# A vision-transformer tower on one core: image tiles asked for at the start and pooled between the parts of the weight preparation, the two layers' weights turned behind the first planes

## The chip, the cores and the metric

The kernel runs on 1 core of one Trainium2 chip, in one launch. The metric is the device time of that launch in microseconds (us), the median of several runs. Engine names: PE or TensorE (matmul), DVE or VectorE, ACT or ScalarE, POOL or GpSimd, SP or SyncE (here it only issues DMAs). ACT issues DMAs too: x tiles go on ACT's queue, all else on SP's.

## The reference

64 images of 12 channels, 224 x 224, float32. Each image becomes T = 196 tokens (14 x 14 patches) of width D = 192, goes through one attention layer over the whole width, a residual, and then an expert layer with its own attention of 12 heads:

```python
pooled = x.reshape(B, C, 14, 16, 14, 16).sum(axis=(3, 5))         # 12 values a token
h = einsum('bcij,ce->bije', pooled, channel_weights)
h = h + attn(layernorm(h), Wq, bq, Wk, bk, Wv, bv)                 # softmax over 196 tokens
# expert layer on layernorm(h): router -> softmax -> top 98 of 196 tokens for each of 4 experts
h1 = expert_sum(mask_e * (layernorm(y) * gamma + beta)) @ w1.T + b1      # 768 hidden + 3 x 192
x_attn = attention(12 heads, q, k, v from h1);  x_mlp = gelu(h1[:768])
out = y + combine(mask_e * (concat(x_mlp, x_attn) @ w2.T + b2)) , the two halves of w2's rows added
```

Since a token is made of 12 values, the kernel folds the weights together first (`Abd`, `WR`, `G4`, `WI` for the first attention, `M` for the product with w1) and works on 25 numbers per token up to `M`.

## The kernel before, in words

**Stages.** The program has a preparation, a prologue for the first group of 8 images, a loop over the groups, and two closing sections. Every engine runs its own list of operations in order, written from tables of (slot, operation): `prologue()`, `opening()` and `body()` make them, and `run` (L601) walks them for each engine. An operation is a pooling piece, a planes product, one round of choosing, and so on. The loop's table (`body`) is the same in both kernels.

**Preparation.** SP asks for 20 weight loads (L652 to L671), w1 (960 KB and a rest of 48 KB), w2 (1440 KB) and the two biases last, all counted on one semaphore `w_in`. PE waits for all 20 and turns the weights with transposes: Wq, Wk, Wv, the router, the centred channel weights, w1 (22 transposes), the summed halves of w2 (16), through four PSUM banks that ACT empties (L739, L1028). Then come small products: `banks[0]` and `banks[1]` from cwcT (L727, L732), the second of which is `Vp`. ACT copies Vp out, SP copies it into the middle rows of `G` with a DMA from SBUF to SBUF (L673; the rows call it hid<-hid), and DVE centres G into `Gc` (L1212 to L1214). PE turns Gc, multiplies it (L744 to L751), DVE makes `A_rep`, `S_rep`, `L` (L1216 to L1229), PE spreads them (L755 to L761), and DVE writes `Abd`, `WR`, `G4`, `WI` (L1234 to L1241). Last, PE multiplies L with the turned w1 into four banks (L767, L769) and ACT copies them out as `M` (L1035). SP waits for the turned w2 and sends the summed b2 as a bias row into w2T (L676, semaphore `bias_in`), and PE waits for M, for DVE's last piece and for bias_in ahead of anything else.

**Tiles of x.** Each group of 8 images is 12 tiles of 1568 KB (112 partitions), loaded into three buffers in turn (`xt`, NX = 3). `load` (L1050) asks for the first three on ACT's queue, behind M's copies; `fetch` (L1055) asks for tile n + 3 when tile n is pooled. DVE pools a tile in seven pieces (`pool`, L1260, reduction at L1267). POOL spreads the sums of a tile (`own_row`, L1513). After three tiles, which are a pair of images m, PE gathers them (`planes`, L786), ACT copies the result, PE makes tokens (`tok`, L796) and DVE copies these (`tok_raw`, L1274). Tiles of the next group are pooled in pieces set between the operations of this one.

**Routing.** After the fourth tok: a layer norm whose power is taken by POOL (L1522, three times), the first attention image by image (first_max L819 and L1308, first_exp L835, first_mix L844), the stream (L853 to L868), the gates (L1361 to L1384), a turn (`gate_rows`, L876, copied to `rows` at L1390), 13 rounds of choosing the 8 largest (L1398, L1403), `chosen`, `spread` (u_tok, L1420 and L1423; the rows call it both<-zs,sel) and `turn_u` (L892). Then the opening: project (L919), hidden for all 8 images (L909), and the first image's 12 peaks (L937 on PE, L1459 on DVE, two banks), and then the loop.

A table entry of the prologue is written like this (m is the pair, t the tile, p the piece):

```python
    for m in range(GRP // PAIR):
        front += pooling(0, m, steadily(TILES * PIECES * m, 1))
    end = TILES * PIECES * GRP // PAIR + 3
    ...
    for m in range(AHEAD):
        front += pooling(1, m, steadily(end + 6 + 0.75 * TILES * PIECES * m, 0.75))
```

## Time and profile before

| what | value |
|---|---|
| median of 3 runs | 1855.82 us (1848.53 to 1863.67) |
| the profiled execution | 1857.67 us |
| its span in the trace | 1855.8 us, 34563 instructions |
| busy PE, PEld, DVE, ACT, POOL | 1525.9, 1252.8, 1215.5, 846.7, 249.2 us |
| chain that ended last | PE 37%, DVE 26%, issue 21%, DMA 7% |
| DMA | 218.03 MB, 117 GB/s in the mean |

Times in rows count from the span's start. PEld is the weight load of a matmul and overlaps PE. In a timeline a row is a start, a busy time, engine and line, the operation, output <- input, how many, and in brackets the idle time before it with what ended it. In the table of windows the columns are named in the rows' group. The granted clock (PEclk) is a share of TensorE's full clock: 1.00 is the level of 2.4 GHz and 0.50 that of 1.2 GHz. The idle time of an engine that nothing waits for costs nothing.

### The profile page before, as it was taken

The numbers are of one execution on the slowest core, as the hardware profiler recorded it, in microseconds if no ns is written. First come the engines' busy times: TensorE is split into PE (matmuls) and PEld (weight loads), VectorE is DVE, ScalarE is ACT, GpSimd is POOL, SyncE is SP. The second block draws the span as 40 slices with busy tenths as digits, with TensorE's granted clock in tenths as the row PEclk, the third lists the DMA queues.
The fourth block names the chain that finished last, engine by engine and source line by source line (L and its number), as shares of the span: only waits on it lengthen the run. The fifth ranks groups of instructions, "written<-read, shape, count | busy, mean of one in ns | idle before, by whom it ended". The sixth has DMA issues, their size and how long they took to land.

```text
span 1855.8 us, 34563 instructions
## 1 busy us (share of the span) xinstructions
PE 1525.9 (82%) x12440; PEld 1252.8 (68%) x12440; DVE 1215.5 (65%) x2822; ACT 846.7 (46%) x1935; POOL 249.2 (13%) x318
## 2 busy tenths in 40 slices
PE   4214188998889898998899898989989899989998
PEld 3103176777777677777777677867777687868786
DVE  3366847785877657784877667784777757573552
ACT  1001054544545455544645455544545456545653
POOL 2002101220012001210012001120022101110000
PEclk8556578999999899998999899997899899999999
DMA  3797635542656155542646155642656152101220
GB/s 77 198 231 186 182 82 143 142 131 64 173 128 175 49 150 145 145 128 71 174 128 166 49 154 141 155 121 57 162 137 173 49 150 50 41 25 43 54 57 15
DMA packets 99598, 218.03 MB, mean 117 GB/s; under 512 B 61371, under 2 KB 75877, under 8 KB 88678
## 3 DMA queue, kind: packets, MB, share of 16 engines
q10 hardware_dynamic: 12288, 154.15, 31.5%
q1 hardware_dynamic: 87142, 61.68, 14.4%
q8 instruction: 102, 1.67, 0.4%
q14 instruction: 66, 0.54, 0.1%
HBM read 186.57 MB, written 28.90 MB: 116 GB/s over the span
## 4 chain that ended last, share of the span: by engine, by line
PE 37%; DVE 26%; issue 21%; DMA 7%; POOL 4%; ACT 3%; SPq 0%; DVEq 0%; ACTq 0%; POOLq 0%
DVE psums L1267 9%; DVE peaks L1459 6%; PE bank L1002 6%; PE bank L909 5%; PE bank L971 4%; DMA xt<-in_x_dram 4%; PE bank L919 3%; POOL var L1522 3%; PE bank L937 3%; DMA qs<-shiftT 3%; PE bank L956 2%; PE bank L835 2%; PE bank L819 2%; DVE rows L1403 2%; DVE top L1398 1%
## 5 line engine op out<-in xcount | busy, mean ns | idle before, releaser
L1459 DVE TENSOR_REDUCE peaks<-bank 98x2 f32<-98x392 f32 x768 | 424.6, 562 | 185.8 <-PE bank L937 164.9
L1155 ACT ACTIVATE Pb<-bank 98x392 f32<-98x392 f32 x768 | 374.7, 497 | 290.7 <-PE bank L956 250.1
L1267 DVE TENSOR_REDUCE psums<-xt 112x2 f32<-112x512 f32 x672 | 430.1, 678 | 74.7 <-DMA xt<-in_x_dram 52.6
L937 PE MATMUL bank<-ks,qs 96*98 96x196 f16 x1536 | 265.4, 259 | 59.5 <-DMA ks<-qk_scratch 31.6
L1002 PE MATMUL bank<-w2T,hid 128*98 128x192 f32 x1536 | 301.9, 335 | 0.0
L956 PE MATMUL bank<-qs,ks 97*98 97x196 f16 x1536 | 267.0, 258 | 9.9 <-DMA qs<-shiftT 9.2
L937 PEld LDWEIGHTS bank<-ks,qs 96*98 96x98 f16 x1536 | 165.8, 127 | 143.0 <-DVE peaks L1459 50.4
L1002 PEld LDWEIGHTS bank<-w2T,hid 128*98 128x98 f32 x1536 | 240.3, 170 | 1.7
L971 PE MATMUL bank<-Pb,vals 98*32 98x196 f32 x3072 | 181.5, 357 | 11.6 <-ACT Pb L1155 11.6
L956 PEld LDWEIGHTS bank<-qs,ks 97*98 97x98 f16 x1536 | 167.5, 130 | 20.1 <-DMA qs<-shiftT 10.7
L1448 DVE TENSOR_TENSOR qk<-bank,qk 96x392 f16<-96x392 f32 x128 | 71.8, 561 | 137.9 <-ACT qk L1142 129.5
L1550 POOL TENSOR_TENSOR fin<-fin,both 98x384 f32<-98x384 f32 x64 | 63.8, 997 | 651.9 <-DVE fin L1484 651.9
L909 PE MATMUL bank<-UT,M 104*128 104x196 f32 x768 | 143.6, 338 | 0.0
L909 PEld LDWEIGHTS bank<-UT,M 104*128 104x128 f32 x768 | 132.6, 197 | 2.6 <-issue 2.2
L971 PEld LDWEIGHTS bank<-Pb,vals 98*32 98x32 f32 x3072 | 84.5, 114 | 72.5 <-issue 48.1
L1133 ACT ACTIVATE hid<-bank 128x392 f32<-128x392 f32 x192 | 93.9, 497 | 83.0 <-PE bank L909 82.5
L1513 POOL TENSOR_TENSOR spread_p<-psums,cst 112x196 f32<-112x196 f32 x96 | 49.9, 520 | 595.7 <-DVE psums L1267 595.3
L786 PE MATMUL bank<-spread_p,cst 112*24 112x196 f32 x192 | 49.2, 406 | 97.9 <-POOL spread_p L1513 97.9
L1067 ACT COPY oT<-bank 128x196 f32<-128x196 f32 x192 | 61.9, 322 | 132.0 <-PE bank L971 127.1
L1002 PE MATMUL bank<-w2T,onT 96*98 96x192 f32 (+1 forms) x512 | 106.7, 331 | 8.5 <-ACT onT L1067 8.5
L919 PE MATMUL bank<-UT,M 104*96 104x196 f32 x512 | 111.8, 368 | 0.1
L786 PEld LDWEIGHTS bank<-spread_p,cst 112*24 112x24 f32 x192 | 20.4, 120 | 118.2 <-issue 112.4
(181 smaller groups left out, 1826.2 us busy)
## 6 DMA issues: line engine op xcount, KB each, us to landing
xt<-in_x_dram ACTq DMA_DIRECT2D x96, 1568.0 KB, 8.9
qk_scratch<-qk SPq DMA_DIRECT2D x64, 294.0 KB, 4.1
qs<-qk_scratch SPq DMA_DIRECT2D x192, 73.5 KB, 2.9
ks<-qk_scratch SPq DMA_DIRECT2D x192, 73.5 KB, 3.0
out_dram<-fin SPq DMA_DIRECT2D x64, 147.0 KB
qs<-shiftT SPq DMA_DIRECT2D x128, 2.3 KB
hid<-in_L_ffn_w_dram SPq DMA_DIRECT2D x1, 1440.0 KB
hid<-in_L_ffn_w_dram SPq DMA_DIRECT2D x1, 960.0 KB
```

Of the source, the lines that this page charges most:

```text
L786: mm = pe.matmul(ps[0:PAIR * C, 0:T], const("plane", PP)[:, PAIR * C * t:PAIR * C * t + PAIR * C], spread_p[:, t, :, :].rearrange("p a b - ...
L909: mm = pe.matmul(ps[:, T * j:T * j + T], M[:, 128 * f:128 * f + 128], UT[:, i, :], start=True, stop=True)
L919: mm = pe.matmul(ps[0:DC, T * c:T * c + T], M[:, f:f + DC], UT[:, i, :], start=True, stop=True)
L937: mm = pe.matmul(peak_ps[s][0:HT, T * q:T * q + T], qs[0:KS, i % NSTACK, h, HT * q:HT * q + HT], ks[0:KS, i % NSTACK, h, :], start=True, s ...
L956: mm = pe.matmul(score_ps[s][0:HT, T * k:T * k + T], ks[:, i % NSTACK, h, HT * k:HT * k + HT], qs[:, i % NSTACK, h, :], start=True, stop=True)
L971: mm = pe.matmul(ps[32 * j:32 * j + 32, 0:T], vals[:, i % 2, q, h, :], Pb[:, (H * i + h) % NP, q, :], start=(q == 0), stop=(q == 1))
L1002: mm = pe.matmul(misc_ps[slot][0:HT, D * h:D * h + D], lhs, w2T[0:w, f, :], start=(f == 0), stop=(f == NF + 1))
L1133: act.activation(hid[:, i, 2 * b:2 * b + 2, :].rearrange("p a b -> p (a b)"), ps[:, 0:2 * T], ACT.Gelu).then_inc(free, 1)
L1155: act.activation(Pb[:, (H * i + h) % NP, :, :].rearrange("p a b -> p (a b)"), score_ps[s][0:HT, 0:2 * T], ACT.Exp, scale=float(DH) ** -0.5 ...
L1267: last = dve.tensor_reduce(psums[:, m % 2, t, 2 * p:2 * p + 2], v[:, 2 * p:2 * p + 2, :, :], AX.XY, ALU.add)
L1448: dve.tensor_tensor(qk16[:, m, 1, :, :].rearrange("p c t -> p (c t)"), misc_ps[slot][0:DC, 0:2 * T], qk16[:, m, 0, :, :].rearrange("p c t ...
L1459: dve.tensor_reduce(peaks[:, h // 6, :, h % 6], peak_ps[s][0:HT, 0:2 * T].rearrange("p (q k) -> p q k", q=2), AX.X, ALU.max, negate=True). ...
```

## The change

What it does:

- Tile 0 of x is asked for as ACT's first act, tiles 1 and 2 when the 15 small weight loads are in. `w_in` now counts 15 loads, and the five of w1, w2, b1, b2 have a semaphore of their own (`w12_in`). Tiles 3, 4 and 5 are asked for by SP, tile 3 ahead of the copy of Vp into G and the other two behind it, each when a buffer has been pooled. `load` is gone.
- DVE pools tile 0 ahead of its first preparation step, tile 1 behind Gc, tile 2 behind L. Its functions for the operations are moved ahead of the preparation in the file, unchanged.
- The turning of w1 and w2 and the products for M leave the preparation and become an operation `fuse` of three parts, which PE and ACT do in the prologue behind the planes of the pairs 0, 1 and 2, and DVE (the sum over w2 and b2) in part 0. They use the score and peak banks. The tok of the first three pairs comes later in the table, behind the fuse.
- SP sends the bias row when all late turns are done. PE waits for M in project and hidden of the prologue and for the bias in hidden.
- The next group's first two pairs are pooled at other slots of the routing, the third within the opening; turn_u comes where the choosing ends.

The core of the diff ("..." marks what is left out):

```diff
-W_LOADS = 20
+W_LOADS = 15
+W12_LOADS = 5
 REPLACED = -1.0
...
-    ops = [("load", 0)]
     front = []
+    pieces = TILES * PIECES
     for m in range(GRP // PAIR):
-        front += pooling(0, m, steadily(TILES * PIECES * m, 1))
-    end = TILES * PIECES * GRP // PAIR + 3
+        for slot, op in pooling(0, m, steadily(pieces * m, 1), True, 1.2 if m == GRP // PAIR - 1 else 7):
+            if op[0] not in ("pool", "fetch") or (op[0] == "pool" and TILES * m + op[3] >= SETUP_TILES) \
+                    or (op[0] == "fetch" and TILES * m + op[3] >= SETUP_TILES):
+                front.append((slot, op))
+    front += [(pieces * (m + 1) + 4, ("fuse", 0, m)) for m in range(3)]
+    end = pieces * GRP // PAIR + 3
     first, at = routing(0, end)
     front += first + [(at + 0.5 * r, ("choose", 0, r)) for r in range(ROUNDS)]
     front += choosing(0, at + 0.5 * ROUNDS + 1)
-    for m in range(AHEAD):
-        front += pooling(1, m, steadily(end + 6 + 0.75 * TILES * PIECES * m, 0.75))
-    front += turning(0, end + 60)
-    return ops + in_order(front) + sum(opening(0, False), [])
+    front += pooling(1, 0, steadily(end + 9, 0.95))
+    front += pooling(1, 1, steadily(end + 29, 0.65))
+    plan = [in_order(front + turning(0, at + 0.5 * ROUNDS + 3))] + opening(0, False)
+    for slot, op in in_slots(pooling(1, 2, steadily(1, 0.24))):
+        plan[min(slot, len(plan) - 1)].append(op)
+    return sum(plan, [])
...
+            sp.wait_ge(pooled, 1)
+            sp.dma_start(xt[:, 0, :], x_tile(0, NX)).then_inc(x_in[0], 16)
             sp.wait_ge(su_act, 2)
             sp.dma_start(G[C:2 * C, :], Vp).then_inc(su_dma, 16)
-            sp.wait_ge(turn_free, NT - 1)
-            sp.wait_ge(su_dve, 4)
+            for t in range(NX + 1, NX + SETUP_TILES):
+                sp.wait_ge(pooled, t - NX + 1)
+                sp.dma_start(xt[:, t % NX, :], x_tile(0, t)).then_inc(x_in[t % NX], 16)
+            sp.wait_ge(late_free, len(late_turns))
+            sp.wait_ge(su_dve, 8)
             sp.dma_start(w2T[DC:DC + 1, NF + 1, :], b2_in[:, 2, :]).then_inc(bias_in, 16)
...
+            def fuse(at, G_, dg, part):
+
+                if part < 2:
+                    if part == 0:
+                        pe.wait_ge(w12_in, 16 * W12_LOADS)
+                    else:
+                        pe.wait_ge(su_dve, 7)
+                    for n_ in range(LATE_W1 * part, LATE_W1 if part == 0 else len(late_turns)):
+                        if n_ >= MISC:
+                            pe.wait_ge(late_free, n_ - MISC + 1)
+                        for src, at_, r, w in late_turns[n_][0]:
+                            mm = pe.transpose(banks[n_ % MISC][0:w, at_:at_ + r], src, ident[0:r, 0:r])
+                        mm.then_inc(late_full, 1)
+                    return
+                pe.wait_ge(late_free, len(late_turns))
+                for n4, (f, end) in enumerate(M_PARTS):
+                    o = banks[n4][0:U, 0:end - f]
+                    for c in range(2):
+                        pe.matmul(o, L[:, c, :, :].rearrange("p e z -> p (e z)"), w1T[:, c, f:end],
+                                  start=(c == 0), stop=False)
+                    mm = pe.matmul(o, const("last", 1), b1_in[:, f:end], start=False, stop=True)
+                mm.then_inc(su_pe, 1)
...
             def hidden(at, G_, dg, i):
+                if at.section == "pro":
+                    pe.wait_ge(su_act, 3)
+                    pe.wait_ge(bias_in, 16)
...
+            act.dma_start(xt[:, 0, :], x_tile(0, 0)).then_inc(x_in[0], 16)
+            act.wait_ge(w_in, 16 * W_LOADS)
+            for t in range(1, NX):
+                act.dma_start(xt[:, t, :], x_tile(0, t)).then_inc(x_in[t], 16)
...
+            def fuse(at, G_, dg, part):
+
+                if part < 2:
+                    for n_ in range(LATE_W1 * part, LATE_W1 if part == 0 else len(late_turns)):
+                        parts, dst = late_turns[n_]
+                        act.wait_ge(late_full, n_ + 1)
+                        act.copy(dst, banks[n_ % MISC][0:parts[0][3], 0:parts[-1][1] + parts[-1][2]]).then_inc(late_free, 1)
+                    return
+                act.wait_ge(su_pe, 10)
+                for n4, (f, end) in enumerate(M_PARTS):
+                    dst, src = M[:, f:end], banks[n4][0:U, 0:end - f]
+                    if f == HID:
+                        dst = dst.rearrange("u (n d h) -> u n h d", d=DH, h=H // 2)
+                        src = src.rearrange("u (n h d) -> u n h d", d=DH, h=H // 2)
+                    last = act.copy(dst, src)
+                last.then_inc(su_act, 1)
...
+            def fuse(at, G_, dg, part):
+                if part == 0:
+                    dve.wait_ge(w12_in, 16 * W12_LOADS)
+                    dve.tensor_tensor(w2_sum, w2_in[:, 0:2, :], w2_in[:, 2:4, :], ALU.add).then_inc(su_dve, 1)
+                    dve.tensor_tensor(b2_in[:, 2, :], b2_in[:, 0, :], b2_in[:, 1, :], ALU.add).then_inc(su_dve, 1)
...
+            first = At("first", 0)
+            for p in range(PIECES):
+                pool(first, 0, 0, 0, 0, p)
...
             dve.tensor_scalar(Gc, G, mean[:, 1:2], None, ALU.subtract).then_inc(su_dve, 1)
+            for p in range(PIECES):
+                pool(first, 0, 0, 0, 1, p)
             dve.wait_ge(su_pe, 5)
             last.then_inc(su_dve, 1)
+            for p in range(PIECES):
+                pool(first, 0, 0, 0, 2, p)
             dve.wait_ge(su_pe, 9)
```

Three places in the order of instructions. First DVE in the preparation (mean and hid are the steps to Gc, psums<-xt the pools of a tile in seven pieces, on_tok and soft the step behind Gc's products, both<-hid the sum over w2, Abd the first of the last step). Before:

```order
L1204 TENSOR_REDUCE mean<-tmp 12x1
L1205 TENSOR_SCALAR mean<-mean 12x1
L1206 TENSOR_SCALAR tmp<-tmp,mean 12x192
L1207 TENSOR_TENSOR both<-hid 96x1920
L1208 TENSOR_TENSOR oT<-oT 1x192
L1209 MEMSET peaks 98x24
L1212 TENSOR_REDUCE mean<-hid 25x1
L1213 TENSOR_SCALAR mean<-mean 25x1
L1214 TENSOR_SCALAR hid<-hid,mean 25x192
L1216 COPY on_tok<-bank 13x8x13
```

With the change:

```order
L1245 TENSOR_REDUCE psums<-xt 112x2 x7
L1501 TENSOR_REDUCE mean<-tmp 12x1
L1502 TENSOR_SCALAR mean<-mean 12x1
L1503 TENSOR_SCALAR tmp<-tmp,mean 12x192
L1504 MEMSET peaks 98x24
L1507 TENSOR_REDUCE mean<-hid 25x1
L1508 TENSOR_SCALAR mean<-mean 25x1
L1509 TENSOR_SCALAR hid<-hid,mean 25x192
L1245 TENSOR_REDUCE psums<-xt 112x2 x7
L1513 COPY on_tok<-bank 13x8x13
```
and, some rows further down,

```order
L1245 TENSOR_REDUCE psums<-xt 112x2 x7
L1533 TENSOR_TENSOR Abd<-bank,cst 128x128
L1534 TENSOR_TENSOR Abd<-Abd,cst 128x128
L1535 TENSOR_TENSOR WR<-bank,cst 128x148
L1537 TENSOR_SCALAR G<-bank,cst 128x192 x4
L1539 TENSOR_TENSOR WI<-bank,cst 24x24
L1540 COPY WI<-cst 24x24
L1245 TENSOR_REDUCE psums<-xt 112x2 x5
L1253 TENSOR_TENSOR both<-hid 96x1920
L1254 TENSOR_TENSOR oT<-oT 1x192
L1245 TENSOR_REDUCE psums<-xt 112x2 x4
L1258 COPY tok_raw<-bank 98x96
```

The pools of three tiles now stand between the steps, and the sum over w2 in the middle of the fourth tile's.

Second PE behind the preparation (spread_p is planes, WI,planesT is tok, hid and both the turning of w1 and w2, hid,P and M,cst the products for M). Before:

```order
L767 MATMUL bank<-hid,P 104x384 x2
L769 MATMUL bank<-M,cst 104x384
L767 MATMUL bank<-hid,P 104x192 x2
L769 MATMUL bank<-M,cst 104x192
L786 MATMUL bank<-spread_p,cst 24x196 x3
L796 MATMUL bank<-WI,planesT 98x48 x2
L786 MATMUL bank<-spread_p,cst 24x196 x3
L796 MATMUL bank<-WI,planesT 98x48 x2
L786 MATMUL bank<-spread_p,cst 24x196 x3
L796 MATMUL bank<-WI,planesT 98x48 x2
```

With the change:

```order
L819 MATMUL bank<-spread_p,cst 24x196 x3
L810 MATMUL bank<-hid,P 104x384 x2
L812 MATMUL bank<-M,cst 104x384
L810 MATMUL bank<-hid,P 104x384 x2
L812 MATMUL bank<-M,cst 104x384
L810 MATMUL bank<-hid,P 104x384 x2
L812 MATMUL bank<-M,cst 104x384
L810 MATMUL bank<-hid,P 104x192 x2
L812 MATMUL bank<-M,cst 104x192
L829 MATMUL bank<-WI,planesT 98x48 x2
L819 MATMUL bank<-spread_p,cst 24x196 x3
L829 MATMUL bank<-WI,planesT 98x48 x2
```

The tok of pair 2 now stands behind all seven rows of the products for M.

Third DVE at the end of the routing and in the opening (sel, zs and both<-zs,sel are chosen and spread, qk the project step, cg and gate the gate8 step). Before:

```order
L1405 TENSOR_SCALAR rows<-rows 32x196
L1267 TENSOR_REDUCE psums<-xt 112x2 x2
L1411 COPY sel<-bank 98x64
L1267 TENSOR_REDUCE psums<-xt 112x2
L1420 TENSOR_TENSOR zs<-z_tok,var 98x16x25
L1423 TENSOR_TENSOR both<-zs,sel 98x16x26 x4
L1267 TENSOR_REDUCE psums<-xt 112x2 x2
L1274 COPY tok_raw<-bank 98x96
L1448 TENSOR_TENSOR qk<-bank,qk 96x392 x4
L1459 TENSOR_REDUCE peaks<-bank 98x2 x8
L1434 TENSOR_TENSOR cg<-sel,prob 98x64
```

With the change:

```order
L1389 TENSOR_SCALAR rows<-rows 32x196
L1395 COPY sel<-bank 98x64
L1404 TENSOR_TENSOR zs<-z_tok,var 98x16x25
L1407 TENSOR_TENSOR both<-zs,sel 98x16x26 x4
L1432 TENSOR_TENSOR qk<-bank,qk 96x392 x4
L1245 TENSOR_REDUCE psums<-xt 112x2 x5
L1443 TENSOR_REDUCE peaks<-bank 98x2 x2
L1245 TENSOR_REDUCE psums<-xt 112x2 x4
L1443 TENSOR_REDUCE peaks<-bank 98x2 x2
L1245 TENSOR_REDUCE psums<-xt 112x2 x4
L1443 TENSOR_REDUCE peaks<-bank 98x2 x2
```

Three pieces around sel and two behind spread are gone, the tok_raw copy too, and 21 pieces stand between the projections and the peaks.

## Rows read from the trace of the kernel before

**Rows 1.** Table of windows: us, PE busy, PEld, DVE, ACT, POOL, PEclk, DMA share, GB/s.

```profile
0.00:20.00 20.00, 0.00 (x0) 0.00 (x0) 6.47 (x9) 1.28 (x1) 12.14 (x6) 1.00 0.71 175
20.00:40.00 20.00, 14.30 (x96) 11.76 (x96) 5.54 (x20) 7.05 (x18) 0.00 (x0) 0.91 0.01 3
40.00:60.00 20.00, 15.68 (x26) 5.80 (x26) 2.27 (x9) 1.76 (x4) 0.00 (x0) 0.50 0.17 45
...
120.00:140.00 20.00, 2.99 (x10) 1.54 (x10) 12.89 (x22) 0.31 (x1) 1.33 (x3) 0.50 1.02 236
...
260.00:265.00 5.00, 5.00 (x37) 4.92 (x35) 3.09 (x10) 3.41 (x8) 0.00 (x0) 1.00 0.02 4
...
400.00:700.00 300.00, 265.57 (x2185) 218.69 (x2184) 209.19 (x495) 151.92 (x345) 35.16 (x46) 0.94 0.47 120
...
1000.00:1300.00 300.00, 266.61 (x2189) 219.31 (x2188) 208.77 (x508) 146.24 (x334) 41.44 (x49) 0.92 0.46 117
```

**Rows 2.** Chain of waits, the copy of Vp into G: start, us, what.

```profile
33.20 2.00 DMA hid<-hid
```

**Rows 3.** Timeline of DVE, pools of the first and the twelfth tile.

```profile
65.25 4.24 DVE L1267 TENSOR_REDUCE psums<-xt 112x2 f32<-112x512 f32 x7 [22.72 <-DMA xt<-in_x_dram]
...
142.26 4.24 DVE L1267 TENSOR_REDUCE psums<-xt 112x2 f32<-112x512 f32 x7 [2.63 <-DMA xt<-in_x_dram]
```

**Rows 4.** DMA issues of the page: count, KB each, median us to landing.

```profile
xt<-in_x_dram ACTq DMA_DIRECT2D x96, 1568.0 KB, 8.9
qk_scratch<-qk SPq DMA_DIRECT2D x64, 294.0 KB, 4.1
```

**Rows 5.** Timeline of PE, preparation: w1 turned, then M's products.

```profile
23.82 5.20 PE L739 MATMUL bank<-cst,hid 128*96 128x128 f32 x22
...
40.12 2.89 PE L767 MATMUL bank<-hid,P 96*104 96x384 f32 x4
...
54.72 0.96 PE L769 MATMUL bank<-M,cst 1*104 1x192 f32 x2
```

**Rows 6.** Timeline of DVE, preparation.

```profile
22.08 2.14 DVE L1207 TENSOR_TENSOR both<-hid 96x1920 f32<-96x1920 f32 x1
...
35.23 0.34 DVE L1212 TENSOR_REDUCE mean<-hid 25x1 f32<-25x192 f32 x1 [10.71 <-DMA hid<-hid]
...
37.34 0.25 DVE L1216 COPY on_tok<-bank 13x104 f32<-13x104 f32 x1 [1.26 <-PE bank L751]
...
40.23 0.29 DVE L1234 TENSOR_TENSOR Abd<-bank,cst 128x128 f32<-128x128 f32 x1 [1.22 <-PE bank L761]
```

**Rows 7.** Timeline of DVE, routing: prob, rows, u_tok.

```profile
204.30 0.22 DVE L1384 TENSOR_TENSOR prob<-soft,red 98x64 f32<-98x64 f32 x1
...
209.09 0.34 DVE L1390 COPY rows<-bank 32x196 f32<-32x196 f32 x1
...
231.32 2.09 DVE L1423 TENSOR_TENSOR both<-zs,sel 98x416 f32<-98x416 f32 x4
```

**Rows 8.** Timeline of PE, planes ahead of turn_u, hidden, the loop's first peak.

```profile
235.34 2.12 PE L786 MATMUL bank<-spread_p,cst 112*24 112x196 f32 x6 [6.43 <-POOL spread_p L1513]
...
238.76 0.89 PE L892 MATMUL bank<-cst,both 98*104 98x98 f32 x4
...
255.16 2.18 PE L909 MATMUL bank<-UT,M 104*128 104x196 f32 x12
...
266.94 0.33 PE L937 MATMUL bank<-ks,qs 96*98 96x196 f16 x2
```

**Rows 9.** Timeline of DVE, opening: a pair of peaks.

```profile
255.18 1.04 DVE L1459 TENSOR_REDUCE peaks<-bank 98x2 f32<-98x392 f32 x2 [1.32 <-PE bank L937]
```

**Rows 10.** Timeline, DMA issues in the loop's first group.

```profile
287.29 0.32 ACTq L1046 DMA_DIRECT2D xt<-in_x_dram  x1
...
289.90 0.31 SPq L683 DMA_DIRECT2D qk_scratch<-qk  x1
...
297.00 0.31 SPq L689 DMA_DIRECT2D qs<-qk_scratch  x1
```

More of the change, by code:

```diff
@@ L116, with pooling @@
 AHEAD = 3
+SETUP_TILES = 3
 FC2 = 6
 MIX_LAG = 5
[L121 removed]
+def pooling(dg, m, at, more=True, turn=1.2):
     ops = []
@@ new lines, in _ @@
+            last.then_inc(su_dve, 1)
+            for p in range(PIECES):
+                pool(first, 0, 0, 0, 2, p)
+            dve.wait_ge(su_pe, 9)
+            done(dve.tensor_tensor(Abd[:, 0, :], banks[1][:, 0:128], const("mask8"), ALU.mult))
+            dve.tensor_tensor(Abd[:, 1, :], Abd[:, 0, :], const("one13"), ALU.add)
+            dve.tensor_tensor(WR[:, :], banks[2][:, 128:276], const("mask4"), ALU.mult)
+            for j in range(QUAD):
+                dve.tensor_scalar(G4[:, j, :], banks[3][:, 128:128 + D], const("col4")[:, j:j + 1], None,
+                                  ALU.mult)
@@ L1493, in _ @@
+            dve.tensor_tensor(WI[:, 0:24], banks[0][0:24, 128:152], const("mask2", 24), ALU.mult)
+            dve.tensor_copy(WI[:, 24:48], ident[0:24, 0:24]).then_inc(su_dve, 1)
+            run(dve, {"fuse": fuse, "pool": pool, "tok": tok, "take": take, "norm1_scale": norm1_scale, "norm1": norm1,
                       "first_max": first_max, "shift1": shift1, "stream": stream, "stream_norm": stream_norm,
```

181 lines of the change are left out of this document (74 added, 107 removed).

## The prediction

> **What bounds the kernel now.** I read the table of windows first. In the first 20 us the DMA engines are busy 0.71 of the time and TensorE does nothing; from 20 to 60 us TensorE is busy 14.30 + 15.68 us and the DMA engines are nearly idle (0.01, then 0.17); from there to about 150 us the DMA engines are full and TensorE is busy 3 of 20 us [rows 1]. So the start is three stages in series: weights in, weights prepared, then the twelve image tiles of the first group. The timeline of DVE shows what the third costs: the first tile is pooled from 65.25, the twelfth from 142.26 to 146.5, so a tile every 7.0 us, of which DVE needs 4.24 [rows 3]. A lone tile lands a median 8.9 us after it is asked for [rows 4]. After the twelfth tile comes the routing, a chain through all engines, where DVE and the order on TensorE end the waits [rows 7, 8]. The loop behind it (the other 86% of the span) has the same tables in both kernels.
>
> **The change part by part.** The sum is made against the profiled execution, 1857.67 us (span 1855.8 and 1.9 around it), 1.9 above the median of the three runs.
>
> *1. Tiles asked for early.* The 40 us in which the DMA engines did little can hold five to six tiles. What they give back depends on how soon DVE frees the three buffers, since the preparation now stands between the pools. The hinge is the small copy of Vp into G, on SP's queue, behind w1, w2 and now behind tile 3 (SP waits for the first pooled tile, asks for tile 3, then for the copy). DVE waits for it, and behind it in DVE's order stand the pools of tiles 1 and 2. If a queue works in order, all that is ahead must be through: the weights, 0.71 x 20 = 14.2 us of engine time [rows 1], four tiles of 7.0 us, 28.0 (three of them share the engines from the other queue), 2 us until the first request runs, and the copy's own 2.0 us [rows 2]: V = 46 us. Before, it had landed by 35.2 [rows 6]. If nothing ahead holds it: the first tile lands at 2 + 8.9 us and is pooled by about 16, and from the end of w1's turning (29.0 [rows 5]) to the copy's landing (35.2) there were 6.2 us, with the two products in them, plus one of slack: V = 23. Those are the bounds. I take 46: a write on SP's queue has its readers issued 7.1 us later when a tile is in flight on ACT's queue [rows 10], against a median of 4.1 [rows 4], so the small one does wait for the large one's bytes, even from another queue.
>
> No row shows a small copy behind a tile on one queue. The Trainium skill (DMA: Bandwidth & Descriptors, Queues, rings and completion order) has it that SP and ACT own one ring each on every engine, consumed in ring order, with the engines going round the rings packet by packet; by it V is 46 and not 23. That rule speaks against placing tile 3 ahead of the copy.
>
> From V on, in DVE's order: mean and Gc 0.9 (35.23 to 36.1), pool tile 1 4.2, A_rep to L 1.7 (37.34 to 39.0), pool tile 2 4.2, Abd to WI 2.3 (40.23 to 42.5) [rows 6]: V + 13.3. Tile 3: seven pieces of 0.6 and between them the sum over w2, 2.1 and 0.3: V + 19.9. TensorE starts the first planes at V + 13.4 and 2.1 us later the 22 transposes of w1. They took 5.20 us [rows 5] with the clock granted in full; at half it would be 10.4; I take 8, as their surroundings now are mostly idle: V + 23.5. The fetch of tile 6 is behind their copies on ACT, so it goes out at V + 24.1 and lands at V + 33.0, tiles 7 and 8 at V + 40.0 and V + 47.0. Tile 8 is pooled at V + 51.2. Its planes take 2.8 with POOL's step, and behind them TensorE runs the products for M: 40.12 to 55.7, 15.6 us [rows 5]. Only then comes that pair's tok, 1.4 with its planes' copy long done, for which DVE waits at the second piece of tile 10. Twelve pieces are behind this wait, 7.2 us: tile 11 is pooled at V + 78.2 = 124.4, where it was 146.5. **Gain 22.1.** With V = 23 the tiles set the pace: tile 3 lands at 44, tile 8 at 79, and with the same 27.0 behind its pool at 83.3 the twelfth is pooled at 110.3, a gain of 36.2.
>
> *2. Fewer pools in the routing.* 63 pieces stood there and 42 do now. Up to the gates 46 become 39; these 4.2 us lie where DVE waits for TensorE, POOL or ACT (planes(1,0) moves from the fourth first_exp to the end of the eighth), so I count 0 of 4.2. Between prob (204.5) and rows (209.09) stood 4.6 us, since planes and tok were ahead of gate_rows on TensorE; now three pieces, 1.8: 2.7 gained. Nine pieces between the choosing rounds go, 5.4, a tok_raw of 0.3 comes: 5.1. Three around sel go, 1.8, of which 0.3 was cover: 1.5 [rows 7]. Then planes and tok (235.34) no longer stand ahead of turn_u: u_tok was done at 233.4, turn_u began at 238.76 [rows 8]: 5.4. **Gain 14.7**; bounds 10 and 19.
>
> *3. The third pooling goes into the opening.* 21 pieces of 0.6 are 12.5 us of DVE, in slots of 2.35 us in which DVE had 1.04 us of work and 1.32 idle [rows 9]. A slot with four pieces needs 3.4, 1.1 too long; two peak banks let TensorE run one pair ahead, no more. Laid out slot by slot (five pieces hidden behind the first two images, then 4, 4, 4, 4 and the five gate8 operations) the last peaks come some 4 to 5 us late, and planes(1,2) with tok stand before the loop's first peak: 266.94 [rows 8] comes 6.5 later than it otherwise would. **Loss 6.5**; bounds 0 (all covered) and 12.5 (none).
>
> *4. The rest.* w1, w2 turned later, the bias copy and its wait: ACT and SP have nothing else there, and hidden asks for the bias some 100 us after it is sent. Cost 0; if the cover is gone it shows as part of term 1. The M copies hold the fetch of tile 12 back by about 12 us, but its first piece is due 15 us after tile 11. Tiles 21 to 23 are fetched in the opening and not before it; they are due from the loop's first slots on, and the q and k copies beside them may wait 3 to 4 us, with a full image of slack.
>
> Sum: 1857.67 - 22.1 - 14.7 + 6.5 = **1827.4**, I say 1827.
>
> **The rivals.** *A, the small copy isn't held.* V = 23 as above, 36.2 instead of 22.1: 1813. For it: it has 12 rows only. Against it: the write that waits [rows 10]. *B, the opening loses the clock.* At 260 us TensorE has the full clock with no gaps [rows 1]; where DVE now makes it wait, it may fall to half, and six more batches of hidden of 2.18 us [rows 8] take twice that, 12 us more: 1839. Against it: the gaps are about 1 us. *C, slower: the loop's mean clock.* It was granted 0.94 from 400 to 700 and 0.92 from 1000 to 1300 for the same work [rows 1]. The loop would start at another point against the throttle. Were it 0.03 lower over its 1500 us and TensorE the bound all through, 1500 x 0.03 / 0.94 = 48 us: 1875. It decides from 0.02 on (32 us, the whole gain). Against it: the two stretches carry 2185 and 2189 matmuls in equal time, so 0.02 of clock cost nothing there. *D, the products for M run at the full clock.* They take 7.8, not 15.6; then the last tile's landing at V + 68 bounds, and tile 11 is pooled 5.9 earlier: 1821.5. Against it: in the window of 40 to 60 us TensorE is busy 15.68 us in one piece at 0.50 [rows 1]. The Trainium skill (TensorE: Matmul & The Clock Gate, Part 1) says that the throttled state is the default and sustained activity releases it; by that these products would be released, and the sum would be 1821.5; the trace of before disagrees with 0.50 throughout.
>
> That the change does not do what it says has one place: w_in shares the engines with tile 0. Priced in V, since the total of bytes counts there and not the start.
>
> **How the numbers follow.** Forecast 0.52 (own range 1817 to 1838), A 0.20, D 0.10, B 0.13, C 0.05. A and D lie under 1837, which is 1% below the median and about what a measurement of this kernel can tell from no change (its three runs lie within 0.4% of the median); the forecast does in nearly all of its range, B in a third: faster 0.83, within 1% 0.13, slower 0.04. The range 1803 to 1843 leaves C out, takes A and B in, and the bounds of terms 2 and 3.
>
> **What would show it.** Right: the copy into G lands at 43 to 48 with the DMA engines full before it and idle for some 5 us after; tok_raw of the third pair waits for TensorE for about 9 us; tile 11 pooled near 124; turn_u directly after u_tok; peaks in the opening waiting for DVE. Wrong: Gc before 30 us (A), the products for M at 1.00 (D), hidden at 0.50 (B), a clock under 0.92 in the loop (C).

## The result and the profile after

The changed kernel took 1829.43 us, the median of four runs (1813.34 to 1834.04). The kernel before, beside it, took 1858.82 (1848.53 to 1863.67, four runs). The ratio is 0.9845, with a 95% interval of 0.9802 to 0.9887. Predicted were 1827 and a range of 1803 to 1843. The profiled execution took 1830.25 us (span 1828.5); it is set against the profiled 1857.67 of before.

The table of windows of the changed kernel answers to [rows 1]: us, PE busy, PEld, DVE, ACT, POOL, PEclk, DMA share, GB/s.

```profile
0.00:20.00 20.00, 4.21 (x26) 3.83 (x26) 11.54 (x20) 2.66 (x6) 12.65 (x7) 1.00 0.98 227
20.00:40.00 20.00, 2.59 (x12) 1.50 (x11) 0.00 (x0) 0.50 (x2) 0.00 (x0) 1.00 1.03 261
40.00:60.00 20.00, 7.05 (x37) 4.93 (x38) 17.06 (x43) 1.09 (x3) 1.04 (x2) 1.00 0.61 162
60.00:80.00 20.00, 8.23 (x45) 5.79 (x43) 16.98 (x30) 4.62 (x10) 2.08 (x4) 0.59 0.88 231
80.00:100.00 20.00, 10.15 (x18) 3.67 (x18) 11.67 (x20) 0.31 (x1) 1.56 (x3) 0.50 1.00 250
100.00:120.00 20.00, 11.04 (x28) 5.31 (x26) 8.34 (x16) 2.08 (x5) 1.04 (x2) 0.50 0.63 166
```

The DMA engines are full up to 40 us and busy 0.61 of the time from there to 60, where before they were nearly idle from 20 to 60 us (0.01 and 0.17). The price is in the second row: DVE does nothing in it. The timeline of DVE in the changed kernel says why, and where the start ends (the step to Gc; then the first pieces of tile 10, the tok that waits, the last twelve pieces):

```profile
42.77 0.34 DVE L1507 TENSOR_REDUCE mean<-hid 25x1 f32<-25x192 f32 x1 [26.96 <-DMA hid<-hid]
...
99.42 1.28 DVE L1245 TENSOR_REDUCE psums<-xt 112x2 f32<-112x512 f32 x2 [3.08 <-DMA xt<-in_x_dram]
108.08 0.26 DVE L1258 COPY tok_raw<-bank 98x96 f32<-98x96 f32 x1 [7.38 <-PE bank L829]
108.26 7.20 DVE L1245 TENSOR_REDUCE psums<-xt 112x2 f32<-112x512 f32 x12
...
216.69 2.46 DVE L1245 TENSOR_REDUCE psums<-xt 112x2 f32<-112x512 f32 x4 [0.15 <-DVE peaks L1443]
219.07 1.03 DVE L1443 TENSOR_REDUCE peaks<-bank 98x2 f32<-98x392 f32 x2
220.02 2.46 DVE L1245 TENSOR_REDUCE psums<-xt 112x2 f32<-112x512 f32 x4
```

DVE waits 26.96 us for the small copy of Vp, then 7.38 us for the products for M, and has pooled the twelfth tile at 115.46 (146.5 in [rows 3]). The last three rows are in the opening: four pieces and two peaks fill a slot and leave no gap, where [rows 9] had 1.32 us. The timeline of PE has the other side of each:

```profile
58.11 3.95 PE L803 MATMUL bank<-cst,hid 128*96 128x128 f32 x22
...
91.91 2.89 PE L810 MATMUL bank<-hid,P 96*104 96x384 f32 x4
...
106.51 0.96 PE L812 MATMUL bank<-M,cst 1*104 1x192 f32 x2
...
193.80 0.87 PE L925 MATMUL bank<-cst,both 98*104 98x98 f32 x4 [3.26 <-DVE both L1407]
...
219.69 0.84 PE L975 MATMUL bank<-ks,qs 96*98 96x196 f16 x4 [0.45 <-DVE peaks L1443]
220.37 2.23 PE L945 MATMUL bank<-UT,M 104*128 104x196 f32 x12
224.46 0.84 PE L975 MATMUL bank<-ks,qs 96*98 96x196 f16 x4 [1.86 <-DVE peaks L1443]
225.15 2.23 PE L945 MATMUL bank<-UT,M 104*128 104x196 f32 x12
...
229.79 0.33 PE L994 MATMUL bank<-qs,ks 97*98 97x196 f16 x2
```

turn_u stands directly behind u_tok. In the opening PE now waits for DVE's peaks, 1.86 us at the worst place. The last row is the loop's first score, here the mark of the loop's start. Before it stood at 267.12, so the start is 37.3 us shorter, and yet the execution only 27.4: from the first score to the end it took 1598.7 us, and before 1588.7.

### The profile page after: what moved, and what is told of

The parts are those of the page before. It is cut to its first block, busy times and chain, and to the rows that moved or that the text cites. A ratio compares the mean times of both kernels' runs of the same rounds, so it can differ in the third digit from the quotient of the medians.

```text
span 1828.5 us, 34571 instructions
## 1 busy us (share of the span) xinstructions
PE 1542.0 (84%) x12440; PEld 1263.2 (69%) x12440; DVE 1216.9 (67%) x2822; ACT 848.5 (46%) x1935; POOL 249.3 (14%) x318
## 4 chain that ended last, share of the span: by engine, by line
PE 36%; DVE 28%; issue 21%; DMA 6%; ACT 4%; POOL 4%; SPq 1%; DVEq 0%; ACTq 0%; POOLq 0%
DVE psums L1245 10%; DVE peaks L1443 7%; PE bank L1040 6%; PE bank L945 4%; PE bank L1009 4%; PE bank L957 3%; POOL var L1572 3%; DMA qs<-shiftT 3%; PE bank L975 3%; PE bank L994 2%; PE bank L868 2%; PE bank L852 2%; DVE rows L1387 2%; PE bank L1018 1%; DVE qk L1432 1%
## 5 line engine op out<-in xcount | busy, mean ns | idle before, releaser
L975 PE MATMUL bank<-ks,qs 96*98 96x196 f16 x1536 | 269.5, 262 | 63.4 <-DMA ks<-qk_scratch 32.9
L994 PE MATMUL bank<-qs,ks 97*98 97x196 f16 x1536 | 270.7, 261 | 11.1 <-DMA qs<-shiftT 10.6
L994 PEld LDWEIGHTS bank<-qs,ks 97*98 97x98 f16 x1536 | 170.0, 132 | 21.6 <-DMA qs<-shiftT 12.2
L957 PE MATMUL bank<-UT,M 104*96 104x196 f32 x512 | 113.4, 372 | 0.2
L957 PEld LDWEIGHTS bank<-UT,M 104*96 104x96 f32 x512 | 90.3, 187 | 9.2 <-issue 4.6
L1572 POOL TENSOR_TENSOR var<-var,cst 98x16 f32<-98x16 f32 x24 | 69.7, 2903 | 183.2 <-DVE var L1278 110.9
```

What stands on the lines that cost most here:

```text
L957: mm = pe.matmul(ps[0:DC, T * c:T * c + T], M[:, f:f + DC], UT[:, i, :], start=True, stop=True)
L975: mm = pe.matmul(peak_ps[s][0:HT, T * q:T * q + T], qs[0:KS, i % NSTACK, h, HT * q:HT * q + HT], ks[0:KS, i % NSTACK, h, :], start=True, s ...
L994: mm = pe.matmul(score_ps[s][0:HT, T * k:T * k + T], ks[:, i % NSTACK, h, HT * k:HT * k + HT], qs[:, i % NSTACK, h, :], start=True, stop=True)
L1572: gp.tensor_tensor(var[:, 2, :], var[:, 1, :], const("half", HT), ALU.pow).then_inc(gp_pow, 1)
```

## The experiments

Nine variants of the changed kernel were measured, and the two kernels as they were three times more. The table has the marks of each profile, from the same timelines. Experiments 6, 8 and 9 and the changed kernel's third time ran on one chip, the rest on another; of the first profile of either kernel the record does not name the chip. Experiments 1 to 6 and the second "before" are one run each. "Loop" is the span less the first score, PE its busy time in the loop.

| kernel | step to Gc | 12th tile pooled | turn_u | first score | loop | PE |
|---|---|---|---|---|---|---|
| before | 35.2 | 146.5 | 238.8 | 267.1 | 1588.7 | 1424.9 |
| before, again | 34.5 | 136.8 | 230.5 | 259.0 | 1592.9 | 1433.0 |
| changed | 42.8 | 115.5 | 193.8 | 229.8 | 1598.7 | 1437.2 |
| changed, second time | 42.6 | 114.8 | 193.4 | 230.8 | 1591.5 | 1431.2 |
| changed, third time | 42.5 | 116.7 | 195.2 | 232.4 | 1588.1 | 1426.7 |
| 1 copy ahead of tile 3 | 37.3 | 110.2 | 187.7 | 223.9 | 1592.9 | 1433.9 |
| 2 copy ahead of w1 | 30.6 | 113.4 | 191.5 | 230.0 | 1589.2 | 1428.5 |
| 3 tok ahead of M | 42.8 | 108.2 | 187.6 | 226.7 | 1583.3 | 1420.1 |
| 4 second half as before | 42.4 | 116.3 | 208.8 | 238.3 | 1598.4 | 1436.0 |
| 5 third pooling in the gaps | 42.6 | 115.3 | 194.0 | 232.1 | 1588.3 | 1423.1 |
| 6 the same, one fetch held | 42.2 | 114.7 | 192.4 | 232.1 | 1586.4 | 1427.8 |
| 7 = 2 + 3 + 5 | 30.0 | 104.6 | 184.6 | 222.8 | 1591.2 | 1426.8 |
| 8 = 1 + 3 + 6 | 38.0 | 104.5 | 182.6 | 221.4 | 1595.8 | 1437.7 |
| 9 = 8, fetches behind q and k | 37.0 | 104.6 | 182.1 | 213.5 | 1599.5 | 1438.5 |

**1 and 2. What holds the small copy.** The copy of Vp goes ahead of tile 3 in the first, and ahead of w1, w2, both biases and tile 3 in the second.

```diff
-            sp.wait_ge(pooled, 1)
-            sp.dma_start(xt[:, 0, :], x_tile(0, NX)).then_inc(x_in[0], 16)
             sp.wait_ge(su_act, 2)
             sp.dma_start(G[C:2 * C, :], Vp).then_inc(su_dma, 16)
+            sp.wait_ge(pooled, 1)
+            sp.dma_start(xt[:, 0, :], x_tile(0, NX)).then_inc(x_in[0], 16)
```

> SP asks for the copy of Vp into G ahead of tile 3; nothing else differs from the changed kernel, where the copy is issued at 23.0 us and DVE gets it at 42.8. Theory Q (the queue's order holds the copy: it waits for all bytes ahead of it on SP's queue, now without tile 3's 7 us): DVE's Gc step starts at 35 to 37 us. Rival R (the engines' whole load holds it, whatever its place): still 42 to 43. With Q the twelfth tile is pooled at 109 us instead of 115.5, since everything on DVE hangs on the copy; with R it stays within 1 us. The first score matmul of the loop moves by as much.

> SP asks for the copy of Vp ahead of w1, w2, b1, b2 and tile 3 (the requests of the big weights now come at about 23 us instead of 10 to 14). Q: the copy has nothing ahead of it on its queue and Gc starts at 25 to 28 us, slowed a little by tiles 1 and 2 on the other queue. R: not before 29, when those two tiles are through. For the end it gains no more than the run with the copy ahead of tile 3 alone, for then the DMA engines are full from the start and tile 8 lands at 78 in both: twelfth tile pooled at 108 to 110. If the copy were the bound throughout it would be near 100.

Measured: 1818.61 us and 1821.07 us, one run each (before beside them 1860.56). Timeline of DVE in the first, the step to Gc:

```profile
37.28 0.34 DVE L1507 TENSOR_REDUCE mean<-hid 25x1 f32<-25x192 f32 x1 [21.65 <-DMA hid<-hid]
```

Timeline of DVE in the second, the same step and the first pieces of tile 3:

```profile
30.56 0.34 DVE L1507 TENSOR_REDUCE mean<-hid 25x1 f32<-25x192 f32 x1 [15.02 <-DMA hid<-hid]
...
50.80 3.06 DVE L1245 TENSOR_REDUCE psums<-xt 112x2 f32<-112x512 f32 x5 [7.03 <-DMA xt<-in_x_dram]
```

And SP's issues of the copy, first in the changed kernel, then in the second of these:

```profile
22.96 0.85 SPq L692 DMA_DIRECT2D hid<-hid  x1
```

```profile
22.69 0.87 SPq L685 DMA_DIRECT2D hid<-hid  x1
```

It is issued at the same time in both, so the difference is transfer. From issue to DVE's step it takes 19.8 us in the changed kernel, 14.5 without tile 3 ahead of it (that is 37.28 less an issue at 22.79) and 7.9 without w1 and w2 ahead. On idle engines it took 2.0 [rows 2]. So tile 3 ahead costs it 5.3 us and w1 and w2 ahead 6.6; 5.9 are left, with nothing ahead on its own queue and two tiles of ACT's queue in flight.

The first experiment ends rival R as written (still 42 to 43 us). The second does not: the step came at 30.56, not at the 25 to 28 of theory Q, and R had said "not before 29, when those two tiles are through". The DMA queues of the second between 23.0 and 27.9 us (packets, MB, share of the 16 engines; q10 is ACT's queue, whose packets are a tile's 14 KB, and q1 is SP's) show the part that theory Q lacked:

```profile
q10 hardware_dynamic: 82, 1.15, 98.2%
```

The copy was issued at 22.69 with nothing ahead on its queue, and up to 27.9 not one packet of SP's queue was moved; the first starts at 27.99, 5.3 us after the issue. ACT's queue met the same in the changed kernel: its tiles 1 and 2, issued from 14.91 on while w1 and w2 were in flight, have no packet until 20.28. Once both queues are being served, they take turns. The same view of the changed kernel between 20.5 and 26.0 us:

```profile
q10 hardware_dynamic: 81, 1.16, 79.7%
q1 hardware_dynamic: 80, 0.31, 19.7%
```

Equal packets, but of 14 KB for the tiles and 3.8 KB for w1 and w2, so that the weights got about a fifth of the bytes.

Of the 5.5 us in the first all but 0.2 reach the twelfth tile. Of the 12.2 in the second only 2.0 do: tile 3 is then behind the weights, DVE waits 7.03 us for it, and the transfers set the pace. The changed kernel's own three profiles lie 1.9 us apart at that mark, so the 5.3 is clear of this spread and the 2.0 is not. Of the three places tried, the best is behind the weights and ahead of the tile.

**3. The tok of pair 2 ahead of the products for M.**

```diff
-        for slot, op in pooling(0, m, steadily(pieces * m, 1), True, 1.2 if m == GRP // PAIR - 1 else 7):
+        for slot, op in pooling(0, m, steadily(pieces * m, 1), True, 1.2 if m >= GRP // PAIR - 2 else 7):
```

> The tok of pair 2 stands ahead of the products for M on TensorE, not behind them; the rest as in the changed kernel. My theory: the 7.4 us in which DVE waits for this tok (100.7 to 108.1) go, and what bounds then is the landing of tile 11 at about 106.5: pooled at 110.8, 4.7 us earlier than 115.5. Rival: the products are only moved against the next wait, and the planes of the fourth pair wait for TensorE instead: twelfth tile pooled earlier, but its tok no earlier than 119, gain under 1 us at the loop's first score.

Measured 1811.77 us in its one run. The twelfth tile is pooled at 108.2, 7.3 us earlier (4.7 were expected; tile 11 lands by 103.96 and not at 106.5), and turn_u comes 6.2 earlier; the rest is a longer wait for the last tok (5.15 us for 4.27), since M's products, moved behind that tok, end only at 109.9 and hold back the last planes. Its opening was 3.1 us longer than the changed kernel's, and the timeline of PE shows why:

```profile
218.36 1.03 PE L975 MATMUL bank<-ks,qs 96*98 96x196 f16 x4 [1.85 <-DVE peaks L1443]
219.19 4.18 PE L945 MATMUL bank<-UT,M 104*128 104x196 f32 x12
```

Behind the wait of 1.85 us for DVE the batch of hidden took 4.18 us, against 2.23 in the changed kernel's own profile above: the granted clock was 0.50 there, and 1.00 in the other. The same batch took 3.91 and 3.70 in the two repeats of the changed kernel, and 4.26 in experiment 2; only in experiment 1 was it 2.23 again.

**4. The routing and the opening as before.** The front part of the change stays, the pooling of the second group is laid out as it was.

```diff
-    front += pooling(1, 0, steadily(end + 9, 0.95))
-    front += pooling(1, 1, steadily(end + 29, 0.65))
-    plan = [in_order(front + turning(0, at + 0.5 * ROUNDS + 3))] + opening(0, False)
-    for slot, op in in_slots(pooling(1, 2, steadily(1, 0.24))):
-        plan[min(slot, len(plan) - 1)].append(op)
-    return sum(plan, [])
+    for m in range(AHEAD):
+        front += pooling(1, m, steadily(end + 6 + 0.75 * pieces * m, 0.75))
+    front += turning(0, end + 60)
+    return in_order(front) + sum(opening(0, False), [])
```

> The next group's three poolings and turn_u at the slots of the kernel before; the early tiles and late turning stay. My theory (terms 2 and 3): from the twelfth tile pooled to turn_u it is 92 us again (78.3 in the changed kernel, 92.2 before), and from turn_u to the loop's first score 28.4 again (36.0 in the changed one): the first score comes 6.3 us later than in the changed kernel, at 236. Rival: the routing's gain comes from the earlier start (tiles already in) and not from the table: then it stays at 78 to 82 and the first score comes earlier than in the changed kernel.

Measured 1838.48 us. From the twelfth tile to turn_u 92.5 us (before 92.3 and 93.7, changed 78.3 to 78.6), from there to the first score 29.6 (before 28.4, changed 36.0 to 37.4). Both are back, and the planes and tok stand ahead of turn_u again in the timeline of PE:

```profile
205.34 2.13 PE L817 MATMUL bank<-spread_p,cst 112*24 112x196 f32 x6 [6.44 <-POOL spread_p L1561]
207.96 0.86 PE L827 MATMUL bank<-WI,planesT 24*98 24x48 f32 x4 [0.49 <-ACT planesT L1104]
208.76 0.89 PE L923 MATMUL bank<-cst,both 98*104 98x98 f32 x4
```

**The kernel before once more,** for the spread.

> The kernel before, unchanged, for one more trace. From the loop's first score to the end of the span it took 1588.7 us before and 1598.7 in the changed kernel, whose loop is the same program. Theory L (the loop's own spread, which goes with the granted clock, 0.94 against 0.92 to 0.93): this run lies anywhere from 1585 to 1605, with the clock. Rival M (the change costs the loop 10 us by where its transfers fall): 1587 to 1591 again.

Measured 1853.72 us. The loop took 1592.9, inside the 1585 to 1605 of theory L and 1.9 above the 1587 to 1591 of rival M; one more trace does not decide between them. What I had not expected was in the start: turn_u came 8.3 us earlier than in the first profile of the same instructions. Its table of windows:

```profile
80.00:100.00 20.00, 2.99 (x10) 1.54 (x10) 13.57 (x23) 0.31 (x1) 1.82 (x4) 0.50 1.02 254
100.00:120.00 20.00, 3.78 (x13) 2.00 (x14) 12.99 (x22) 0.31 (x1) 1.81 (x4) 0.50 1.00 252
120.00:140.00 20.00, 4.33 (x15) 1.87 (x12) 12.99 (x22) 0.62 (x2) 1.56 (x3) 0.50 1.02 266
```

The engines are as full as in [rows 1] (1.02), but they move 252 to 266 GB/s instead of 236; the twelve tiles came 6.2 us apart (63.89 and 70.08 the first two) and not 7.0.

**5. The third pooling in the idle time.** Five pieces go behind spread, seven between the projections, nine into the opening, so that no slot holds four.

```diff
-    for slot, op in in_slots(pooling(1, 2, steadily(1, 0.24))):
+    turn = at + 0.5 * ROUNDS + 3
+    far = turn + 10
+    third = pooling(1, 2, [turn - 0.5] * 5 + [turn + 1.2] * 7 + [far + k for k in (1, 1, 2, 2, 3, 3, 4, 4, 4)])
+    front += [(slot, op) for slot, op in third if slot < far]
...
+    for slot, op in in_slots([(slot - far, op) for slot, op in third if slot >= far]):
```

> The third pooling of the next group put where DVE is idle: 5 pieces between spread and the first projection, 7 between the two projections, 9 in the opening's slots 1 to 4. My theory: DVE's load per slot in the opening is what costs the 7.6 us (turn_u to first score 36.0 against 28.4 before). With 2 to 3 pieces a slot it is under the slot's 2.35 us or just over it: 29 to 31 us, so the first score comes 5 to 7 us earlier. Rival: planes and tok of the third pair on TensorE are what costs: then 34 or more.

Measured 1822.22 us, and turn_u to first score 38.2, not 29 to 31. In the timeline of PE:

```profile
213.30 0.89 PE L979 MATMUL bank<-ks,qs 96*98 96x196 f16 x4 [4.63 <-DMA ks<-qk_scratch]
213.99 4.10 PE L949 MATMUL bank<-UT,M 104*128 104x196 f32 x12
```

and in that of ACT:

```profile
200.43 0.32 ACTq L1102 DMA_DIRECT2D xt<-in_x_dram  x1
```

The 38.2 alone would fit the rival (34 or more), but the longest wait is for a transfer and not for planes and tok. A tile pooled earlier frees its buffer earlier, and its successor is fetched at 200.43, ahead of the q and k loads of the first image. These wait 4.63 us, and the batch of hidden behind the wait runs at half the clock (0.51 granted from 213.3 to 218).

**6. The same with that fetch held** to the opening's third slot.

```diff
+    third = [(far + 2 if op[0] == "fetch" and op[3] == 0 else slot, op) for slot, op in third]
```

> The third pooling laid out as in the run before it (5 pieces behind spread, 7 between the projections, 9 in the opening), where turn_u to the loop's first score took 38.2 us. Now the fetch that the tile pooled between the projections sets off is held until the third slot of the opening, behind the q and k loads of the first two images. Theory T (what ate the gain was that transfer: it went out at 200.43, 3 us ahead of the q and k loads, PE waited 4.63 us for ks and then ran its next batch of hidden in 4.10 us instead of 2.18, at half the clock): the wait for ks falls under 0.5 us, every batch of hidden takes 2.2 us, and turn_u to first score is 29 to 31 us. Theory P (12 pieces between the projections slow the chain by themselves): 35 us or more, with PE waiting for DVE there. Start up to turn_u as in the changed kernel (193 to 194). Time about 7 us under the changed kernel's by T.

Measured 1820.31 us, turn_u to first score 39.7. The first wait is gone, every batch of hidden takes 2.18 to 2.26, and the opening's last step is done by 224, 31.3 us behind turn_u at its start. Then, in the timeline of PE:

```profile
231.75 0.56 PE L980 MATMUL bank<-ks,qs 96*98 96x196 f16 x2 [7.71 <-DMA ks<-qk_scratch]
```

Two tiles asked for at 207.86 and 210.04 were in flight when the second image's q and k loads were issued (209.44 to 211.67). By its number this would be theory P (35 or more), but PE waits for ks and not for DVE. So theory T names the right thing, but not one transfer's worth of it: take away one wait for ks, and the next image's shows.

**7. All three, in the form known then** (2 + 3 + 5), beside the changed kernel, six runs each.

> The copy of Vp ahead of w1, the tok of pair 2 ahead of the products for M, and the third pooling in DVE's idle time. If the three gains add up: twelfth tile pooled near 103 (12 us earlier), the opening 6 us shorter, first score near 211.5 instead of 229.8, and the time 18 us under the changed kernel's, about 1811. If they hide each other, the first score is at 218 or later and the time about 1818.

> The changed kernel again, timed in five rounds. If the gain is what the start gives (37.4 us at the loop's first score): ratio 0.980. If the loop gives 10 us back systematically: 0.985.

Measured 1824.41 us (1815.78 to 1834.64), ratio 0.9842 (0.9796 to 0.9888), and 1822.84 (1817.01 to 1831.31), ratio 0.9832 (0.9787 to 0.9877). No gain, although the loop starts 8.0 us earlier in the profile (222.8 against 230.8; I had expected 211.5, and the opening's wait for ks was 4.66 us again). The changed kernel's ratio lies between the two that were set for it, 0.980 and 0.985, and decides nothing.

**8. The better place for each** (1 + 3 + 6).

> Three edits together: the copy of Vp ahead of tile 3 (which took the twelfth tile from 115.5 to 110.2), tok of pair 2 ahead of the products for M (to 108.2), and the third pooling with the fetch held. If they add: twelfth tile at about 103, turn_u at 182, first score at 211 to 213, which is 17 to 19 us ahead of the changed kernel (229.8, 230.8). Theory L (the loop's length, 1583 to 1599 us in ten traces, goes with TensorE's granted clock and not with where the loop starts): span 211 + 1591, median near 1804, ratio to the kernel before 0.973 to 0.977. Theory M (the loop gives back what the start gains): loop over 1600 us, median near 1820.

> The changed kernel unaltered beside it, as the yardstick: median 1818 to 1830, twelfth tile at 114 to 116, first score at 229 to 231, loop 1585 to 1600 us.

Measured 1821.21 us (1811.74 to 1825.73), ratio 0.9814 (0.9767 to 0.9860), and 1820.82 (1816.38 to 1824.37), ratio 0.9814 (0.9770 to 0.9857). The twelfth tile and turn_u are where they were expected (104.5, 182.6), 12 us ahead of the changed kernel. The wait for ks in front of the loop (6.89 us) took the first score to 221.4, not 211 to 213.

**9. The fetches behind the q and k loads of the second image.**

```diff
-    third = [(far + 2 if op[0] == "fetch" and op[3] == 0 else slot, op) for slot, op in third]
+    third = [(far + 5 if op[0] == "fetch" and op[3] < 2 else slot, op) for slot, op in third]
```

> As the kernel with three edits before it (copy ahead of tile 3, tok of pair 2 ahead of M's products, third pooling spread out), but the first two of the opening's three fetches go out in its sixth slot, behind the q and k loads of the second image. There the last batch of the opening ended 31.4 us behind turn_u, and the loop's first peak then waited 6.89 us for ks, while two tiles (1568 KB each) were on the queues. Theory T (the wait is those two tiles' transfer and nothing else): no wait for ks over 1 us at the loop's first peak, turn_u to first score 31 to 33 us, first score at 213 to 216, loop 1583 to 1599 us, span 1796 to 1815, median near 1806. Theory S (the transfers only come in front of the next image's q and k): first score the same, but waits for ks of 4 us and more in the loop's first 30 us, and the loop 1595 us or longer.

Measured **1810.79 us** (1805.93 to 1815.90), ratio 0.9750 (0.9698 to 0.9801). In the timeline of PE no wait stands ahead of the loop any more:

```profile
211.11 2.26 PE L950 MATMUL bank<-UT,M 104*128 104x196 f32 x12
213.20 0.33 PE L989 MATMUL bank<-cst,peaks 98*6 98x98 f32 x2
213.37 0.33 PE L980 MATMUL bank<-ks,qs 96*98 96x196 f16 x2
213.54 0.33 PE L999 MATMUL bank<-qs,ks 97*98 97x196 f16 x2
...
254.87 0.56 PE L980 MATMUL bank<-ks,qs 96*98 96x196 f16 x2 [4.42 <-DMA ks<-qk_scratch]
```

Theory T holds for the opening: turn_u to first score is 31.4 us, and nothing waits for ks up to 254.87, 41 us into the loop, a wait that the changed kernel had too (4.38 us at 265.15). But the loop took 1599.5, which is theory S's "1595 or longer" and just over the 1583 to 1599 of theory T, so in the loop the two are not told apart. Its slowest run is faster than the fastest of the changed kernel's second and third measurements (its first had one of 1813.34). The third's median is 10 us above it. But the two are from two sets of runs. By the scatter of the runs alone the 10 us are good to some 5; by the ratios to the kernel before, whose intervals overlap a little, the difference is 12 us, give or take 13.

**Where the loop's time goes.** In fourteen traces (those above and the first two) the loop took 1583.3 to 1599.5 us with the same work. It goes with PE's busy time in it, 1420.1 to 1438.5, with a correlation of 0.93 and some 0.8 us for each us; the mean granted clock is 0.93 or 0.94. The two profiles of before take 1588.7 and 1592.9, the three of the changed kernel 1598.7, 1591.5 and 1588.1. So the 10 us by which its first loop was longer than that of before lie within what the same instructions do from run to run (1588.1 to 1598.7). But this isn't all. If each run started its loop where its profile did (less the 1.8 us around the span), the medians give loops of 1597.8, 1590.2 and 1586.7 for the changed kernel and 1599.8, 1598.0 and 1595.5 for experiments 7, 8 and 9. Their granted clock over the whole run is lower too, 0.897 to 0.907 against 0.905 to 0.912 in one set, 0.902 to 0.909 against 0.909 to 0.915 in another. So their starts gained 8, 11 and 19 us in the marks, and against the changed kernel beside them (the second and third time) their loops seem to give back 9 to 11, with a lower clock in experiments 7 and 8. This is not shown: each figure rests on the start of one profile, two profiles of the kernel before differ by 8.1 us there, and the changed kernel's first set gives 1597.8 itself. What brings the clock down is open: the single runs of 1 to 6 do not show it, and where the loop starts was not varied alone.

## Why the prediction was right, point by point

**The kind of start (the first part).** Right: three stages in series became two, and the DMA engines' idle 40 us went.

**Term 1, tiles asked for early: 22.1 predicted, 31.0 between the two profiles.** The way was right and the sizes were off.
- V was taken as 46 and was 42.8, from a copy that is held by what is ahead of it on its own queue, and by the tiles of the other, as argued. The mis-sized term was the tile: 7.0 us each, where the 261 GB/s of the window from 20 to 40 us make 6.2, and with four tiles of 6.2 the same sum gives 43.0. Experiments 1 and 2 show the parts, and rival A (nothing holds it, V = 23) is dead: even with nothing ahead on its queue the step came at 30.6. The Trainium skill (DMA: Bandwidth & Descriptors, Queues, rings and completion order) has one ring per queue on each engine, gone through in ring order, and the engines taking turns between the rings; the steps of 5.3 and 6.6 us for what is ahead in the same queue agree with it, and so do the 81 and 80 packets of the two queues between 20.5 and 26.0 us. It does not account for the 5.3 us in which the copy of experiment 2, alone on its ring, got no turn at all; what sets them is open.
- The 22 transposes were priced at 8 us, between 5.2 and 10.4. They took 3.95. The mis-sized term was first the clock: their surroundings are idle, and I took that for a clock below full. It was granted in full (1.00 from 58.1 to 62.1 us, and 0.50 from 66 on). But before they took 5.20 at the full clock too, so 1.25 us are not the clock, and no run shows what they are.
- From V + 19.7 the fetch of tile 6 is earlier by 4.4 us, 4.1 of which this frees, and tile 8 landed at V + 42.1, where V + 47.0 was predicted. 3.2 of V and 4.9 of this make 8.1 of the 8.9 us.
- The wait for M's products was 7.38 us (predicted some 9), and they took 15.6 at 0.50. Rival D (the full clock, 7.8 us) is dead.
- But the second profile of before shows the term's yardstick moving: its twelfth tile was pooled at 136.8. Against it the gain is 21.1 us (the three of the changed kernel at 115.7 in the mean). The 7.0 us of a tile, on which "before" rested, was the slow end of 6.2 to 7.0.

**Term 2, fewer pools in the routing: 14.7 predicted, 13.9 measured** (twelfth tile to turn_u, 92.26 less 78.34), and 14.2 against experiment 4 (92.49). Counting the 4.2 us up to the gates as nothing, and only what ends a wait, was right. The marks of DVE say it part by part: twelfth tile to prob 57.8 us in both kernels, prob to rows 4.8 and 2.2, rows to sel 20.7 and 15.2, sel to turn_u 9.0 and 3.2.

**Term 3, the third pooling in the opening: 6.5 predicted, 7.6 measured,** 8.7 and 9.0 in the repeats. The slot by slot sum was right. Left out was that a wait of 1.85 us for DVE can take the clock to half for a batch. That is rival B, priced at 12 us for six batches; it came for one batch, 1.5 and 1.7 us, in two of the three profiles of the changed kernel. And "the q and k copies may wait 3 to 4 us, with a full image of slack" is right for the changed kernel and wrong as soon as the pooling is spread better: DVE's lateness is what keeps the fetches behind the q and k loads there. With DVE's load gone (experiments 5 and 6) the same loads were waited for, 4.6 and 7.7 us. So 4.6 of the 7.6 could be avoided, but only together with two fetches (experiment 9: 31.4 us for 36.0). Of the 3.0 that stay over the 28.4 of before, 1.7 are the planes and tok that now stand there (1.18 and 0.54 us in experiment 9), and 1.1 lie ahead of the first image's peaks, where hidden's first batches took 5.0 us and before 4.4.

**Term 4, the rest at nothing.** No wait for the turned w1, w2 or the bias ends last anywhere in the changed kernel's timelines.

**Rival C, the loop's clock.** The loop was 10.0 us longer in the profile, which took back the 8.9 us that term 1 had too little. So that the total, 1827 against 1829.43, is closer than its terms is luck: they give 1820.4 (1857.67 less 31.0 and 13.9, plus 7.6) with the loop as before. The two later sets of the changed kernel, 1822.84 and 1820.82, lie nearer to that than to 1827. Whether the change itself costs the loop anything, as rival C has it, is open; the 48 us that it named did not come.

## What to carry to other kernels

A small copy that a chain waits for goes ahead of the large transfer on its queue, and not ahead of what the next step needs; and its price is not 2 us as long as the other queue keeps the engines full (7.9 us here with nothing ahead on its own). Before a step of an engine is moved into another's idle time, look at the transfers that it sets off: here 21 pieces of pooling were free in the gaps, and only the place of two fetches decided whether 7 us were won. A gain in a short start of a long kernel is read from marks in the trace, with repeats of both kernels, since the loop of one and the same kernel differed by 10.6 us between three profiles, and by 16 over all fourteen.
